# Block 0's first write: scaled sums, one exponent product and one low part made on GpSimd instead of VectorE

## The reference

```python
def rat_write(res, y, wod_w, wab_w, wab_b, du_w, du_b):
    o_d = y @ wod_w.T
    A_B = y @ wab_w.T + wab_b
    out, delta_low = o_d[..., :H], o_d[..., H:]
    ...
    delta = jax.nn.softplus(delta_low @ du_w.T + du_b)
    A_neg = -jax.nn.softplus(A_logit)
    A_bar = jnp.exp(delta * A_neg)
    B_bar = (A_bar - 1.0) / (A_neg - SSM_EPS) * B_proj
    B_bar_skip = delta * B_skip
    A_full = jnp.concatenate([A_bar, jnp.ones_like(A_bar[..., :1])], axis=-1)
    B_full = jnp.concatenate([B_bar, B_bar_skip], axis=-1)
    return (hs * A_full + out * B_full).reshape(b, l, H * C)

def rat_read(res, W, gamma, beta, num_outputs):
    y = jnp.einsum('blhc,hoc->bloh', x, W)
    mu = y.mean(-1, keepdims=True)
    var = y.var(-1, keepdims=True)
    yn = (y - mu) * jax.lax.rsqrt(var + EPS)
    ...
```

## Time and profile before

| | |
|---|---|
| median of three runs | 2254.82 us |
| the profiled execution | 2261.7 us |
| its span, first to last instruction | 2259.8 us |
| mean granted TensorE clock | 0.949 |
| TensorE matmul busy | 1991.6 us, 88% |
| VectorE busy | 1420.5 us, 63% |
| GpSimd busy | 424.1 us, 19% |
| block 0's first write | 882.45 to 993.47 us of the span |

### The profile page before, as it was taken

One profiled execution on the slowest core, in us unless ns is written; L12 is line 12 of the kernel. 1 busy time (PEld: TensorE's weight loads), 2 busy tenths in 40 slices (PEclk: granted clock), 3 DMA queues, 4 the chain that ended last, 5 costly groups with the idle time before them and its releaser, 6 DMA issues.

```text
span 2259.8 us, 25093 instructions
## 1 busy us (share of the span) xinstructions
PE 1991.6 (88%) x9562; PEld 1384.6 (61%) x9562; DVE 1420.5 (63%) x1567; ACT 982.4 (43%) x1378; POOL 424.1 (19%) x325
## 2 busy tenths in 40 slices
PE   2689987899999996269989999999999989989998
PEld 0144455566666653247767777677777677766786
DVE  3666767677777763966845747847738657668200
ACT  3556752478888875126135243035332153341100
POOL 0000004475555570000000001110001100011011
PEclk9799997699999997679999999999999999999999
DMA  8847445576666753135745856965657766578676
GB/s 204 168 106 170 94 109 186 204 273 238 240 239 239 259 183 130 74 137 194 269 190 203 293 198 177 283 222 209 256 196 215 225 230 249 212 224 262 155 175 141
DMA packets 180731, 453.83 MB, mean 201 GB/s; under 512 B 64128, under 2 KB 64384, under 8 KB 165248
## 3 DMA queue, kind: packets, MB, share of 16 engines
q1 hardware_dynamic: 146400, 313.50, 41.7%
q0 software_dynamic: 32480, 128.46, 20.3%
q10 hardware_dynamic: 1728, 10.22, 1.3%
HBM read 304.80 MB, written 147.32 MB: 200 GB/s over the span
## 4 chain that ended last, share of the span: by engine, by line
PE 43%; DVE 6%; ACT 5%; DMA 4%; issue 2%; SPq 0%; POOL 0%; DVEq 0%; POOLq 0%; ACTq 0%
PE ps L1770 16%; PE ps L1582 8%; PE ps L1584 7%; PE ps L1583 7%; DMA sign_h<-sign_h_scratch 3%; ACT L1799 1%; PE ps L1641 1%; DMA up<-up_s_scratch 1%; PE ps L1650 1%; PE ps L1602 1%; DVE Y L2089 1%; PE ps L1691 1%; PE ps L1679 1%; DVE E_attn L2005 0%; ACT E_attn L1823 0%
## 5 line engine op out<-in xcount | busy, mean ns | idle before, releaser
L1770 PE MATMUL ps<-XH,sign_h 128*128 128x512 f32 x768 | 305.3, 398 | 10.1 <-DMA sign_h<-sign_h_scratch 9.8
L1770 PE MATMUL ps<-XL,sign_h 128*128 128x512 f32 x768 | 299.5, 390 | 0.0
L1148 DVE TENSOR_REDUCE maxes<-ps 128x1 f32<-128x512 f32 (+3 forms) x384 | 207.7, 554 | 103.3 <-PE ps L959 78.8
L1582 PE MATMUL ps<-ZH,up 128*128 128x512 f32 x512 | 207.6, 405 | 10.2 <-DVE ZL L2116 8.9
L1583 PE MATMUL ps<-ZL,up 128*128 128x512 f32 x512 | 203.5, 397 | 0.0
L1584 PE MATMUL ps<-ZH,up 128*128 128x512 f32 x512 | 203.4, 397 | 0.0
L1071 ACT ACTIVATE probs<-ps 128x512 f32<-128x512 f32 (+3 forms) x384 | 167.5, 486 | 54.8 <-PE ps L984 32.1
L1770 PEld LDWEIGHTS ps<-XH,sign_h 128*128 128x128 f32 x768 | 144.1, 188 | 55.1 <-issue 13.4
L956 PE MATMUL ps<-turned_k,turned_q 96*128 96x512 f32 (+3 forms) x384 | 159.4, 429 | 12.0 <-DVE maxes L1148 11.2
L1000 PE MATMUL ps<-probs,v_ones 128*64 128x512 f32 (+3 forms) x768 | 169.6, 520 | 0.3 <-ACT probs L1071 0.3
L1770 PEld LDWEIGHTS ps<-XL,sign_h 128*128 128x128 f32 x768 | 144.2, 188 | 31.3 <-issue 1.9
(11 more groups left out here) (333 smaller groups left out, 4183.6 us busy)
## 6 DMA issues: line engine op xcount, KB each, us to landing
sign_h<-sign_h_scratch SPq DMA_DIRECT2D x256, 256.0 KB, 3.8
up<-up_s_scratch SPq DMA_DIRECT2D x58, 1024.0 KB, 6.5
proj<-proj_s_scratch SPq DMA_DIRECT2D x58, 640.0 KB, 4.0
X<-in_x POOLq DMA_DIRECT2D x16, 1024.0 KB, 15.5
xn_scratch<-X SPq DMA_DIRECT2D x16, 1024.0 KB, 14.2
sign_raw<-in_sign SPq DMA_DIRECT2D x32, 512.0 KB, 7.9
sign_h_scratch<-sign_high SPq DMA_DIRECT2D x32, 512.0 KB, 4.0
sign_l_scratch<-sign_low SPq DMA_DIRECT2D x32, 512.0 KB, 5.1
```

The costliest lines, as they stand in the source:

```text
L1148: eng.tensor_reduce(MAXES[:, e, q, k0 // T:k0 // T + 1], ps[:, MX[m % 2], 0:w], AX.X, ALU.max).then_inc(mx_read.sem, mx_read.unit)
L1582: eng.matmul(out_ap, lh, rh, start=start, stop=False, skip_group_check=True)
L1770: mm = eng.matmul(ps[:, sign_bank(m)], s[q][:, f], x[:, n], start=n + w == 0, stop=n == NF - 1 and w == len(operands) - 1, skip_group_chec ...
```

## The change

In block 0's first write alone GpSimd computes six results that VectorE computed: the scaled sums of channels 1 and 2 (into own tiles `OG_first`), the two steps of channel 3's, the product for the third exponent, and block 1's y_low. A new semaphore `og` tells VectorE that a scaled sum is there. On GpSimd they stand between the existing transfers. `small_lows` of block 1 moves on VectorE from behind channel 2's Y to behind channel 3's. The semaphores `sq` and `rs` are merged into one, `sq_rs`, with the same meanings of the waits.

```diff
-        first = [attn, mlp[0], attn, attn]
+        first = [{**attn, "OGP": [in_b(f"OG_first{c}", 8 * c - 8, [P, HC, T]) for c in range(1, C)]}, mlp[0], attn, attn]
...
+                    def og_first(c):
+                        out = tiles["OGP"][c - 1][:]
+                        if c == 1:
+                            eng.wait_ge(xr.sem, xr.at(turn(0, 0), 10))
+                        if c < 3:
+                            eng.tensor_tensor(out, O1[:], bc(tiles["RG"][:, c], HC), ALU.mult).then_inc(og.sem, og.unit)
+                        else:
+                            eng.wait_ge(sk.sem, sk.at(turn(0, 0)))
+                            eng.tensor_tensor(out, O1[:], tiles["DL"][:], ALU.mult).then_inc(og.sem, og.unit)
+                            eng.wait_ge(og.sem, og.at(k=C - 1))
+                            eng.tensor_tensor(out, out, bc(tiles["SK"][:], HC), ALU.mult).then_inc(og.sem, og.unit)
+
+                    def e_in_first():
+                        eng.wait_ge(e_read.sem, e_read.at(turn(0, 0), 1))
+                        eng.tensor_tensor(tiles["E0"][:], tiles["DL"][:], bc(tiles["SP"][:, 2], HC), ALU.mult).then_inc(e_in.sem, e_in.unit)
+
+                    def y_low_first():
+                        eng.wait_ge(yh.sem, yh.at(1))
+                        eng.tensor_tensor(YL[1][:], YIN[:], YH[1][:].bitcast(F32), ALU.subtract).then_inc(yl.sem, yl.unit)
+
                     for c in range(3):
                         load_h(0, c)
                     load_y(1)
                     load_walls(0)
+                    og_first(1)
+                    e_in_first()
                     store_h(0, 0)
+                    og_first(2)
                     load_h(0, 3)
+                    y_low_first()
+                    og_first(3)
                     for c in range(1, C):
                         store_h(0, c)
...
+                    made = "OGP" in tiles
+                    if made and c:
+                        OG = tiles["OGP"][c - 1]
+                        eng.wait_ge(og.sem, og.at(k=c if c < 3 else C))
                     if c < 3:
-                        in_turn(TTo(OG[:], o, bc(tiles["RG"][:, c], HC), ALU.mult))
+                        if not (made and c):
+                            in_turn(TTo(OG[:], o, bc(tiles["RG"][:, c], HC), ALU.mult))
...
-                        if c == 0:
+                        if c == 0 and not made:
                             TTo(E[0][:], DL[:], bc(tiles["SP"][:, 2], HC), ALU.mult).then_inc(e_in.sem, e_in.unit)
...
-                        in_turn(TTo(OG[:], o, DL[:], ALU.mult))
+                        if not made:
+                            in_turn(TTo(OG[:], o, DL[:], ALU.mult))
...
-                        in_turn(TTo(OG[:], OG[:], bc(SK[:], HC), ALU.mult))
+                        if not made:
+                            in_turn(TTo(OG[:], OG[:], bc(SK[:], HC), ALU.mult))
...
-                        if v == 0 and c == 0:
-                            take_y(1)
-                        if v == 0 and c == 2:
-                            small_lows(SM0[1], 1, 0, small_0)
+                    if v == 0:
+                        small_lows(SM0[1], 1, 0, small_0)
```

More of the change, by code:

```diff
@@ L1324, in block_phase @@
         e_in, rg_e_out, e_read, wr = (ev(n, per=k) for n, k in (("e_in", 3), ("rg_e_out", 4), ("e_read", 3), ("wr", 4)))
-        y, ym, yc, sq, yv, rs, z, zh, zl = (ev("r_" + n, per=k) for n, k in
-            (("y", 5), ("ym", 2), ("yc", 2), ("sq", 2), ("yv", 2), ("rs", 2), ("z", 2), ("zh", 2), ("zl", 2)))
+        y, ym, yc, sq_rs, yv, z, zh, zl = (ev("r_" + n, per=k) for n, k in
+            (("y", 5), ("ym", 2), ("yc", 2), ("sq_rs", 4), ("yv", 2), ("z", 2), ("zh", 2), ("zl", 2)))
+        og = ev("og", per=C)
         up_in, proj_in = ([ev(f"{n}_in{a}", per=NM // 2, unit=16) for a in range(2)] for n in ("up", "proj"))
@@ L1506, in first_add @@
                         add(u, 0)
+                    tiles = first[0]
+                    def og_first(c):
[15 more added lines that the diff above has]
+                        eng.tensor_tensor(YL[1][:], YIN[:], YH[1][:].bitcast(F32), ALU.subtract).then_inc(yl.sem, yl.unit)
                     for c in range(3):
@@ L1645, in read @@
                         eng.wait_ge(yc.sem, yc.at(v, 2 if v == 1 else o + 1))
-                        eng.wait_ge(sq.sem, sq.at(v, o + 1))
+                        eng.wait_ge(sq_rs.sem, sq_rs.at(v, o + 1))
                         if v == 1 and o:
-                            eng.wait_ge(rs.sem, rs.at(v, 1))
+                            eng.wait_ge(sq_rs.sem, sq_rs.at(v, 3))
                         for hc in range(HC):
@@ L1671, in second_write @@
                     else:
-                        eng.wait_ge(rs.sem, rs.at(1, 2))
+                        eng.wait_ge(sq_rs.sem, sq_rs.at(1, 4))
                     eng.wait_ge(small_1.sem, small_1.at(u))
@@ L1707, in inner @@
                                 eng.wait_ge(zl.sem, zl.at(v, o + 1))
-                                eng.wait_ge(rs.sem, rs.at(v, o + 1))
+                                eng.wait_ge(sq_rs.sem, sq_rs.at(v, o + 3))
                             else:
@@ L1893, in first_write @@
                         eng.wait_ge(yc.sem, yc.at(v, o + 1))
-                        eng.activation(first[v][f"E{o}"][:], Y[v][:, o], ACT.Square).then_inc(sq.sem, sq.unit)
+                        eng.activation(first[v][f"E{o}"][:], Y[v][:, o], ACT.Square).then_inc(sq_rs.sem, sq_rs.unit)
                         yield
@@ L1902, in first_write @@
                         eng.wait_ge(chain.sem, chain.next())
-                        eng.activation(R[v][:, o], R[v][:, o], ACT.Exp, scale=-0.5).then_inc(rs.sem, rs.unit)
+                        eng.activation(R[v][:, o], R[v][:, o], ACT.Exp, scale=-0.5).then_inc(sq_rs.sem, sq_rs.unit)
                         yield
```

## The result

The changed kernel takes 2266.5 us, the median of 19 runs, against 2255.19 us of 19 runs of before: ratio 1.0036, with a 95% interval of 1.0022 to 1.0051. That is 8.1 us more (5.0 to 11.5), where 9.9 were forecast. The ratio is an estimate from all 19 runs of each kernel and not the quotient of the two medians, which would be 1.0050, or 11.3 us more. The change is slower clear of noise, and by the ratio it lies within 0.5%, though the interval reaches just past that.

A forecast was written before the change was run, and what follows sets the result against it. VectorE alone was taken to bound block 0's first write. With 15.9 us taken from it and 25.8 us of waiting for GpSimd added, +9.9 us on the median 2254.8 gave 2264.7 us (+0.44%), range 2255 to 2272.

The forecast's parts named there:

- The bound: Block 0's first write, 908.95 to 967.34 us: VectorE alone sets the end; TensorE's sum of Y waits 25.13 us.
- What is taken from VectorE: Block 0's first write: exponent product 2.21, y_low 2.89, two scaled sums 2.31 each, low parts and channel 3 6.20; 15.9 us.
- What GpSimd needs: Six new GpSimd instructions in block 0's first write, each at the subtraction's 4.55 us: 27.3 us.
- The lower bound of 3.61: Five of GpSimd's six at 3.61 us, the price of a product with a single broadcast value: 22.6 us in all.
- Turns: In that stretch VectorE and GpSimd take turns on SBUF inputs; each GpSimd instruction costs VectorE 4.30 us, six 25.8.
- the rival in which it gives nothing (+11.4): No overlap at handovers between VectorE and GpSimd: six cost 27.3 us, +11.4 to +11.8, 2266.4 us; 20 in 100.
- Side by side: Rival: both engines run at once in block 0's first write, all 15.9 us gained, 2238.9 us; one in ten.
- Channel 0's Y instructions, left open: Eight Y instructions with one SBUF tensor, 3.25 us; no row showed whether GpSimd holds them, so freedom stayed in the range.
- Order of the turns: Block 0's first write: y_low ends about 941, channel 3's steps 948 and 954, walls 957 before the read at 977; none late.
- The sum: Whole kernel: −15.9 + 25.8 = +9.9 us, from the median 2254.8 to 2264.7 us, +0.44%.
- the faster products: Rival: five GpSimd products take 3.61 us, 4.7 us less, so +5.2 us, 2260.0 us; 13 in 100.
- the free Y instructions: Rival: channel 0's eight Y instructions are not held by GpSimd, saving at most 3.25 us; +6.7, 2261.5 us; 5 in 100.

The follow-up runs named there:

- the one early product: Against before: GpSimd multiplies only out_sb by SK while VectorE waits for ScalarE, small low parts moved as in the change; ratio 0.9997 (0.9983 to 1.0011).
- the run of the order alone: Against before: only the two small low parts moved from behind channel 2's Y to behind channel 3's; ratio 0.9992 (0.9977 to 1.0007).
- the run with one-input products: Against before: VectorE's work untouched, six spare GpSimd products of one tensor with one value per partition added; ratio 1.0083 (1.0056 to 1.011).
- the doubled work: Against before: VectorE keeps everything, GpSimd makes the six results once more into spare tiles nobody reads; ratio 1.0129 (1.0103 to 1.0154).

## Why the prediction was right

**The bound.** That VectorE alone sets the end of block 0's first write held: every run moved the sum of Y by what was added to VectorE or taken from it, and the time followed within its interval, that of the one early product only just.

**What is taken from VectorE.** 15.9 us, not seen apart, but by the difference: 25.7 held less 9.75 net give 15.9. That does not test this term apart from the next ones. What does is that the rows which stay and were not held keep the lengths they had, 2.29 us, 5.39 for eight, and that the moved ones are missing between them. The small low parts fell into the wait for the mean, which gave 1.55 us in the run of the order alone, and in the changed kernel they end at 972.44, 2.54 us before the mean is there.

**What GpSimd needs.** 4.55 us was taken for all six from the subtraction. The product that GpSimd ran free of VectorE took 4.53 us, and the one inside channel 0's Y 4.52. The lower bound of 3.61 for the products fell: that price belongs to one input, as the run with one-input products shows.

**Turns.** 4.30 us each was the price, from handovers seen with VectorE instructions of 128x512; 25.7 us for six is 4.28. So the handover gives its quarter of a microsecond back on 128x2048 too, and the rival in which it gives nothing (+11.4) fell, by the profile. Side by side, the rival on the other side, fell with the first add of 6.47 us and with the doubled work. Channel 0's Y instructions, left open, are held as well: 8.82 us for two of GpSimd's instructions. The remark that every L1137 that met GpSimd's work was stretched is not quite right: the one at 373.53 kept its 0.69 us while a GpSimd instruction started 0.37 us before its end. There VectorE was first and GpSimd's took 1.50 us, where its like take 1.28, so it speaks for the turns all the same.

**Order of the turns.** From the first scaled sum y_low was to end after 32 us and did after 32.2 (932.34); channel 3's steps after 39 and 45, measured 38.8 and 45.4; no scaled sum came late. TensorE's walls took 15.8 us for 15.6 and ended 20 us ahead of the sum of Y.

**The sum.** +9.9 was forecast for the point where the sum of Y starts, and +9.75 came. Not in it is TensorE's clock in the first sum, 1.0 us on top in this profile, which may be chance. The time over 19 runs, +8.1 us, lies under both and holds both in its interval (5.0 to 11.5); whether anything behind the stretch gives 2 us back can't be told from these runs. The same interval also holds +5.2, +6.7 and +11.4, the faster products, the free Y instructions and the handover that gives nothing: it is the profiles that decide between them, not the time. And that the time came out within 0.5% owes something to luck, since the forecast lay 1.4 us under that bound.

## What to carry to other kernels

Moving work from VectorE to GpSimd is no relief where VectorE's remaining instructions read two SBUF tensors: each 128x2048 instruction costs VectorE 4.3 us of standing still to save 2.3. It pays in a gap in which VectorE waits for a third engine (2.3 us in a profile here, too little for the time to show), and ScalarE took eight instructions off VectorE without such a price. Look for instructions that are longer than their own minimum, since such waits are inside the durations and in no row of waits, and try the price on instructions of another stage of the same trace before moving anything.

## What the runs showed of the hardware that was not expected

A GpSimd fill, which reads nothing, left VectorE's two-input instructions at 2.29 us but held its fast one-tensor instructions for its whole length: 6.91 us for eight in place of 3.25, with two fills of 1.84 us in them, and 3.25 again when the fills stood elsewhere. And the same piece of TensorE's work behind a wait varied by 1.5 us: the 16 matmul records of the sum of Y took 8.60 to 10.13 us over the ten profiles, by when the full clock was granted, and 9.01 and 8.60 in the two whose stretch ahead of it was the same.
